# A conditional residual matmul on one core: results stored from a ring of their own, four rows to a partition, and plain copies in place of the residual add

## The chip, the core and the metric

The kernel runs on one core of one Trainium2 chip. The metric is the device time of one execution in microseconds (us), lower is better. Three runs of the kernel before gave a median of 323.65 us.

## The reference

`x` is float32 of shape (128, 128, 1024): 128 samples, 128 channels C, 1024 time steps T. Every sample names one of 8 subjects, and each subject has a 128x128 float32 matrix.

```python
w = weights[subjects]                        # (B, C, D), subjects in 0 .. 7
out = x + jnp.einsum('bct,bcd->bdt', x, w)   # B = C = D = 128, T = 1024
```

The traffic that can't be avoided is 67.1 MB read and 67.1 MB written.

## The kernel before

Two samples (a = 0, 1) make a **tile**: the 64 low partitions (LOW) hold sample a = 0, the 64 high ones (HIGH) sample a = 1, and each partition holds two neighbouring channels of T values (R = 2, a run of 8 KB). Two tiles make a **pair**, which one load of 2 MB brings (line 98) and one store of 2 MB takes away (line 205); there are 64 tiles and 32 pairs. `x_ring` has 12 tile slots, so 6 pairs.

TensorE multiplies a tile in 16 matmuls of 64 rows by 512 columns (line 222): two halves of T, two channels r of each partition, two samples a. The product of sample a lies in its own PSUM tensor of 128x1024 float32, four banks; `product` holds two tiles (PRODUCTS = 2), which is all of PSUM. The columns of the weights are permuted (`bank`, lines 113 and 174), so that the 128 output rows come out as even channels in one half of the partitions and odd ones in the other. This matches two rows to a partition in the store.

The residual is split in two. Where an output row stands in the partitions in which its own x row stands, VectorE (DVE) adds x to the product (`sums`, lines 139 and 140). Where it stands in the other half, x can't be added in place; there the weights hold one more on the diagonal (`add_eye`, line 119), so that TensorE's product is already x plus the einsum, and ScalarE (ACT) only copies it (`cross`, lines 182 and 183). Both write the result over x in `x_ring`. DVE also copies the weights of each tile from `weight_bank` to `weight_ring` (`pick`, line 132), four tiles ahead.

The order is written out by hand, with semaphores. SyncE's queue (SP) issues loads; from the seventh pair on each waits until the store of the pair that had its slots has landed (`x_out`, line 95). ACT issues a pair's store behind its copies, once its own copies and DVE's sums are done (`whole`, lines 187 and 188). TensorE starts tile t when both engines are done with tile t - 2 (`summed`, `copied`) and the load of its pair is in (`x_in`). The first two and the last four tiles are stored one by one, 1 MB each (line 202).

Of the kernel before, what the change touches and what calls it, by code (L numbers as in the profile page):

```python
# [6 lines left out]
DMA_INC = 16  # L7
SLOTS = 12
PAIR = 2
LOADS_AHEAD = 4  # L10
PICK_AHEAD = 4
PRODUCTS = 2


def subject_residual_kernel(nc, x, subjects, weights, out):

# [8 lines left out]
    f32, i32 = mybir.dt.float32, mybir.dt.int32  # L25
    B, C, T = x.shape
    S, _, D = weights.shape
    assert C == D == nc.NUM_PARTITIONS
    H, R = C // 2, 2
    TILES = B // 2  # L30
    LAPS, REST = divmod(TILES, SLOTS)
    assert LAPS and SLOTS % PRODUCTS == 0 and REST % PRODUCTS == 0 and REST == PICK_AHEAD > PRODUCTS
    PAIRS, PAIR_SLOTS = TILES // PAIR, SLOTS // PAIR
    assert SLOTS % PAIR == 0 and REST % PAIR == 0 and LOADS_AHEAD < PAIR_SLOTS
    BANKS = T // PSUM_BANK_COLS

    SINGLE = (*range(PAIR), *range(TILES - REST, TILES))
# [3 lines left out]
    def stores(pairs, place):  # L41

        return sum(PAIR if (pair * PAIR_SLOTS + place) * PAIR in SINGLE else 1 for pair in range(pairs))

    LOW, HIGH = slice(0, H), slice(H, C)
    EVEN, ODD = slice(0, H), slice(H, D)
# [4 lines left out]
    out_of_pair = out.rearrange("(n j a) (h r) t -> n (a h) j (r t)", j=PAIR, a=2, r=R)  # L51

    with ExitStack() as ctx:  # L53
        x_ring = ctx.enter_context(nc.sbuf_tensor("x_ring", [C, SLOTS, R, T], f32))

# [14 lines left out]
        eye_low = ctx.enter_context(nc.semaphore("eye_low"))  # L70
        eye_high = ctx.enter_context(nc.semaphore("eye_high"))
        bank_low = ctx.enter_context(nc.semaphore("bank_low"))
        eyes_added = ctx.enter_context(nc.semaphore("eyes_added"))
# [3 lines left out]
        x_out = [ctx.enter_context(nc.semaphore(f"x_out{s}")) for s in range(PAIR_SLOTS)]  # L77
# [5 lines left out]
        summed = ctx.enter_context(nc.semaphore("summed"))  # L83

        copied = ctx.enter_context(nc.semaphore("copied"))
        block = ctx.enter_context(nc.Block())

        @block.sync
        def _(sp):
            sp.dma_start(weight_halves[:, :, :, :],  # L90
                         weights.rearrange("(i a) (h r) d -> (a h) i (r d)", a=2, r=R)).then_inc(weights_in, DMA_INC)
            for pair in range(PAIRS):
                lap, place = divmod(pair, PAIR_SLOTS)
                if lap:
                    sp.wait_ge(x_out[place], stores(lap, place) * DMA_INC)
                elif place >= LOADS_AHEAD:
                    sp.wait_ge(x_in[place - LOADS_AHEAD], DMA_INC)
# [3 lines left out]
        def _(pool):  # L101
            pool.memset(eye[:, :], 0.0).then_inc(eye_zero, 1)  # L102
            pool.wait_ge(eye_zero, 1)
            for begin, made in ((0, eye_low), (H, eye_high)):
                half = slice(begin, begin + H)
                pool.affine_select(eye[half, :], eye[half, :], pattern=[[-1, H]], base=0, channel_multiplier=1,  # L106
                                   compare_op=mybir.AluOpType.not_equal, fill=1.0).then_inc(made, 1)

        @block.vector
        def _(dve):  # L110
            def bank(half, source, subjects_of):

                return dve.tensor_copy(  # L113
                    weight_bank[half, subjects_of, :, :].rearrange("h i r (q k) -> h i r q k", q=2),
                    weight_halves[source, :, :, :].rearrange("h i r (k q) -> h i r q k", q=2))

            def add_eye(half, row, columns):
                cells = weight_bank[half, :, row, columns]
                return dve.tensor_tensor(cells, cells, eye[half, :].rearrange("h (s k) -> h s k", s=1).broadcast_to(  # L119
                    (H, S, H)), add)  # L120

            def subjects_of(tile):

                _, numbers = nc.values_load_multi_w_load_instructions(  # L124
                    subject_row[0:1, tile * 2:(tile + PICK_AHEAD) * 2], engines=(mybir.EngineType.DVE,), min_val=0,
                    max_val=S - 1, skip_runtime_bounds_check_because="DVE has clamped subject_row to 0 .. S - 1")
                return numbers

            def pick(slot, numbers):

                for subject, half in zip(numbers, (LOW, HIGH)):
                    done = dve.tensor_copy(weight_ring[half, slot, :, :], weight_bank[half, bass.ds(subject, 1), :, :])  # L132
                return done

            def sums(tile, slot):

                low, high = product[slot % PRODUCTS]
                dve.wait_ge(multiplied, tile + 1)
                dve.tensor_tensor(x_ring[LOW, slot, 0, :], low[LOW, :], x_ring[LOW, slot, 0, :], add)  # L139
                dve.tensor_tensor(x_ring[HIGH, slot, 1, :], high[HIGH, :], x_ring[HIGH, slot, 1, :], add).then_inc(summed, 1)  # L140

            dve.sem_inc(summed, PRODUCTS)
            dve.wait_ge(subjects_in, DMA_INC)
            dve.tensor_scalar(subject_row[0:1, :], subject_row[0:1, :], 0, S - 1, mybir.AluOpType.max,  # L144
                              mybir.AluOpType.min).then_inc(clamped, 1)
            dve.wait_ge(weights_in, DMA_INC)
            bank(LOW, LOW, EVENS)
            bank(LOW, HIGH, ODDS).then_inc(bank_low, 1)
            dve.wait_ge(eye_low, 1)
            dve.wait_ge(bank_low, 1)  # L150
            add_eye(LOW, 1, ODD)
            dve.wait_ge(eye_high, 1)
            dve.wait_ge(bank_high, 1)  # L153
            add_eye(HIGH, 0, EVEN).then_inc(eyes_added, 1)
            dve.wait_ge(eyes_added, 1)
            dve.wait_ge(clamped, 1)
            numbers = subjects_of(0)
            for tile in range(PICK_AHEAD):
                pick(tile, numbers[tile * 2:tile * 2 + 2]).then_inc(picked, 1)


            for tile in range(TILES):
                sums(tile, tile % SLOTS)
                ahead = tile + PICK_AHEAD
                if ahead < TILES:
                    if ahead % PICK_AHEAD == 0:
                        numbers = subjects_of(ahead)
                    own = ahead % PICK_AHEAD * 2
                    pick(ahead % SLOTS, numbers[own:own + 2])

        @block.scalar
        def _(act):
            def bank(half, source, subjects_of):
                return act.copy(  # L174
                    weight_bank[half, subjects_of, :, :].rearrange("h i r (q k) -> h i r q k", q=2),
                    weight_halves[source, :, :, :].rearrange("h i r (k q) -> h i r q k", q=2))

            def cross(tile, slot):

                low, high = product[slot % PRODUCTS]  # L180
                act.wait_ge(multiplied, tile + 1)
                act.copy(x_ring[LOW, slot, 1, :], low[HIGH, :])  # L182
                act.copy(x_ring[HIGH, slot, 0, :], high[LOW, :]).then_inc(copied, 1)  # L183

            def whole(tile):

                act.wait_ge(copied, tile + (PRODUCTS + 1))
                act.wait_ge(summed, tile + (PRODUCTS + 1))  # L188
# [3 lines left out]
            act.sem_inc(copied, PRODUCTS)  # L192
            act.wait_ge(weights_in, DMA_INC)
            bank(HIGH, LOW, EVENS)
            bank(HIGH, HIGH, ODDS).then_inc(bank_high, 1)
            for tile in range(TILES):
                slot = tile % SLOTS
                place, j = divmod(slot, PAIR)
                cross(tile, slot)
                if tile in SINGLE:  # L200
                    whole(tile)
                    act.dma_start(out_of_pair[tile // PAIR, :, j, :], x_ring[:, slot, :, :]).then_inc(x_out[place], DMA_INC)
                elif j == PAIR - 1:
                    whole(tile)
                    act.dma_start(out_of_pair[tile // PAIR], x_ring[:, place * PAIR:(place + 1) * PAIR, :, :]).then_inc(
                        x_out[place], DMA_INC)
            for place in reversed(range(PAIR_SLOTS)):
                act.wait_ge(x_out[place], DMA_INC * stores(LAPS + (place < REST // PAIR), place))

        @block.tensor  # L210
        def _(pe):
            def multiply(tile, slot, landed):

                pe.wait_ge(summed, tile + 1)
                pe.wait_ge(copied, tile + 1)
# [10 lines left out]

# [21 lines left out]
```

## Time and profile before

| | us |
|---|---|
| median of 3 runs (323.53 to 324.3) | 323.65 |
| profiled execution, its own time | 323.31 |
| its span, first to last instruction | 321.5 |
| TensorE matmuls busy, 1024 | 243.8 |
| DVE busy, 261 instructions | 196.3 |
| ACT busy, 131 instructions | 132.2 |
| moved by DMA, 134.83 MB, mean | 419 GB/s |
| GpSimd (POOL) busy, 7 instructions | 0.8 |

The span is what the trace covers; the profiled execution's own time is 1.81 us longer, and the median another 0.34 us above that. In the rows below an instruction reads as line, engine, operation, output<-input, partitions x elements, count. "ACTq" and "SPq" rows are the queues' own work, here the issuing of a DMA. A DMA's time in the chain of waits runs from its issue to its landing, so it holds the time that it queued behind other transfers.

### The profile page before, as it was taken

Reading aid. Unit: us, or ns where it says so; the run is one execution under the profiler, and the core shown is the slowest. Engines: PE = TensorE matmul, PEld = TensorE weight load, DVE = VectorE, ACT = ScalarE, POOL = GpSimd, SP = SyncE. Lnnn points to the kernel's source line nnn. Section 1 sums busy time; section 2 is a strip of 40 time slices with the busy share of each in tenths; the row PEclk is TensorE's granted clock in tenths of the full one; section 3 lists DMA queues with packets and bytes.
Section 4 is the critical chain, followed back from the end, with each engine's and each line's share of the span. In section 5 each row is a group of like instructions: output and inputs, shape, how many; then the busy total and the mean of one; then the engine's idle time right before and its main releaser. Section 6 shows DMA issues by size and latency. Waiting matters only on the chain.

```text
span 321.5 us, 2871 instructions
## 1 busy us (share of the span) xinstructions
PE 243.8 (76%) x1024; PEld 112.7 (35%) x1024; DVE 196.3 (61%) x261; ACT 132.2 (41%) x131; POOL 0.8 (0%) x7
## 2 busy tenths in 40 slices
PE   0799997878687866779868698666986868876650
PEld 0344442334343432334424244333333434443320
DVE  3288888637657555764757737567463774755560
ACT  4056566324444242542425525335342553443450
POOL 1000000000000000000000000000000000000000
PEclk9999999979989997997979979998897998999995
DMA  7999999999999999999999999999999999999996
GB/s 287 422 411 427 421 428 425 428 429 429 425 428 428 428 426 428 428 427 427 428 429 428 426 427 430 428 425 428 430 427 426 426 431 428 426 425 432 421 428 271
DMA packets 18024, 134.83 MB, mean 419 GB/s; under 512 B 1105, under 2 KB 1633, under 8 KB 1633
## 3 DMA queue, kind: packets, MB, share of 16 engines
q1 hardware_dynamic: 9232, 67.64, 50.2%
q10 hardware_dynamic: 8784, 67.12, 49.4%
q8 instruction: 2, 0.03, 0.0%
q14 instruction: 6, 0.04, 0.0%
HBM read 67.64 MB, written 67.11 MB: 419 GB/s over the span
## 4 chain that ended last, share of the span: by engine, by line
DMA 73%; PE 17%; DVE 3%; issue 3%; DVEq 1%; ACT 1%; ACTq 0%
DMA out<-x_ring 37%; DMA x_ring<-x 34%; PE product L222 17%; DVE x_ring L140 2%; DMA weight_halves<-weights 1%; ACT weight_bank L174 1%; DVE x_ring L139 1%; DVEq L53 0%; DVEq L124 0%; DVEq L132 0%; DVE weight_bank L119 0%; DVE weight_ring L132 0%; ACTq L188 0%; DVEq L153 0%
## 5 line engine op out<-in xcount | busy, mean ns | idle before, releaser
L222 PE MATMUL product<-x_ring,weight_ring 64*128 64x512 f32 x1024 | 243.8, 630 | 66.1 <-DMA x_ring<-x 43.2
L222 PEld LDWEIGHTS product<-x_ring,weight_ring 64*128 64x128 f32 x1024 | 112.7, 199 | 196.4 <-issue 123.2
L139 DVE TENSOR_TENSOR x_ring<-product,x_ring 64x1024 f32<-64x1024 f32 x64 | 77.9, 1217 | 106.6 <-PE product L222 106.6
L182 ACT COPY x_ring<-product 64x1024 f32<-64x1024 f32 x64 | 64.5, 1008 | 175.5 <-PE product L222 175.5
L140 DVE TENSOR_TENSOR x_ring<-product,x_ring 64x1024 f32<-64x1024 f32 x64 | 78.6, 1228 | 0.8
L183 ACT COPY x_ring<-product 64x1024 f32<-64x1024 f32 x64 | 64.2, 1003 | 0.8
L132 DVE COPY weight_ring<-weight_bank 64x256 f32 x128 | 36.9, 288 | 3.9 <-issue 1.0
L174 ACT COPY weight_bank<-weight_halves 64x1024 f32<-64x1024 f32 x2 | 2.2, 1115 | 2.1 <-DMA weight_halves<-weights 2.1
L144 DVE TENSOR_SCALAR subject_row<-subject_row 1x128 int32<-1x128 int32 x1 | 0.2, 215 | 3.6 <-DMA subject_row<-subjects 3.6
L113 DVE COPY weight_bank<-weight_halves 64x1024 f32<-64x1024 f32 x2 | 1.4, 688 | 0.9 <-DMA weight_halves<-weights 0.9
L174 ACT ACT_TABLE_LOAD x1 | 1.3, 1283 | 1.3 <-PEq L240 1.3
L119 DVE TENSOR_TENSOR weight_bank<-weight_bank,eye 64x512 f32<-64x512 f32 x2 | 1.4, 686 | 0.3 <-ACT weight_bank L174 0.2
L106 POOL TENSOR_SCALAR_AFFINE_SELECT eye<-eye 64x64 f32<-64x64 f32 x2 | 0.5, 234 | 0.3 <-POOL eye L102 0.2
L102 POOL MEMSET eye<- 128x64 f32 x1 | 0.2, 151 | 0.3 <-POOLq L240 0.3
L240 POOL MEMSET const-float32-0.0<- 128x1 f32 x1 | 0.1, 98 | 0.2 <-issue 0.2
L240 POOL MEMSET const-float32-1.0<- 128x1 f32 x1 | 0.1, 98 | 0.0
L240 POOL MEMSET const-bfloat16-1.0<- 128x1 bf16 x1 | 0.1, 98 | 0.0
L240 POOL MEMSET const-uint8-127<- 128x1 uint8 x1 | 0.1, 98 | 0.0
## 6 DMA issues: line engine op xcount, KB each, us to landing
x_ring<-x SPq DMA_DIRECT2D x32, 2048.0 KB, 22.0
out<-x_ring ACTq DMA_DIRECT2D x29, 2048.0 KB, 26.2
out<-x_ring ACTq DMA_DIRECT2D x6, 1024.0 KB, 10.6
weight_halves<-weights SPq DMA_DIRECT2D x1, 512.0 KB, 3.9
subject_row<-subjects ACTq DMA_DIRECT2D x1, 8.0 KB, 2.8
```

Of the source, the lines that this page charges most:

```text
L102: pool.memset(eye[:, :], 0.0).then_inc(eye_zero, 1)
L106: pool.affine_select(eye[half, :], eye[half, :], pattern=[[-1, H]], base=0, channel_multiplier=1, compare_op=mybir.AluOpType.not_equal, fi ...
L113: return dve.tensor_copy(weight_bank[half, subjects_of, :, :].rearrange("h i r (q k) -> h i r q k", q=2), weight_halves[source, :, :, :].r ...
L119: return dve.tensor_tensor(cells, cells, eye[half, :].rearrange("h (s k) -> h s k", s=1).broadcast_to((H, S, H)), add)
L132: done = dve.tensor_copy(weight_ring[half, slot, :, :], weight_bank[half, bass.ds(subject, 1), :, :])
L139: dve.tensor_tensor(x_ring[LOW, slot, 0, :], low[LOW, :], x_ring[LOW, slot, 0, :], add)
L140: dve.tensor_tensor(x_ring[HIGH, slot, 1, :], high[HIGH, :], x_ring[HIGH, slot, 1, :], add).then_inc(summed, 1)
L174: return act.copy(weight_bank[half, subjects_of, :, :].rearrange("h i r (q k) -> h i r q k", q=2), weight_halves[source, :, :, :].rearrang ...
L182: act.copy(x_ring[LOW, slot, 1, :], low[HIGH, :])
L183: act.copy(x_ring[HIGH, slot, 0, :], high[LOW, :]).then_inc(copied, 1)
L222: last = pe.matmul(product[slot % PRODUCTS][a][:, cols], weight_ring[half, slot, r, :], x_ring[half, slot, r, cols], start=r == 0, stop=r ...
L240: nc = bacc.Bacc("TRN2", target_bir_lowering=False, num_devices=1)
```

## The change

- `x_ring` shrinks to 10 tile slots (5 pairs). A new ring, `results`, holds 6 pairs of results, [128, 6, 4, 1024] float32.
- A result pair lies with four channels to a partition (Q = 4), 32 partitions to a sample, so a store of 2 MB takes a run of 16 KB from each of 128 partitions. All pairs are stored whole, the first and the last too.
- The weights get one more on the whole diagonal (one eye of 64 columns for both r, added into `weight_halves` before `bank`), so that x is nowhere added afterwards.
- A tile's product is then taken from PSUM in 8 plain copies of 32 partitions x 1024 columns (a = 0, 1; q = 0 to 3). ACT takes the first 4 of an even tile and the first 5 of an odd one, DVE the other 4 or 3.
- The picking of weights moves from DVE to GpSimd. It runs 5 pairs ahead, held back by `multiplied`.
- A load waits on `picked`, which itself waits on `multiplied` of the pair that had the slots; it waits on no store any more. What waits on a store (`pair_out`) is the first copy of a pair, on ACT and on DVE, from the seventh pair on.

```diff
-SLOTS = 12
+SLOTS = 10
-PICK_AHEAD = 4
+RESULTS = 6
...
+    BLOCKS = [(a, q) for a in range(2) for q in range(Q)]
+    ACT_BLOCKS = (4, 5)
...
-    out_of_pair = out.rearrange("(n j a) (h r) t -> n (a h) j (r t)", j=PAIR, a=2, r=R)
+    out_of_pair = out.rearrange("(n g) (k q) t -> n (g k) (q t)", g=PAIR * 2, q=Q)
...
+        results = ctx.enter_context(nc.sbuf_tensor("results", [C, RESULTS, Q, T], f32))
...
+        def target(tile, a, q):
+
+            pair, j = divmod(tile, PAIR)
+            g = j * 2 + a
+            return results[g * K:(g + 1) * K, pair % RESULTS, q, :]
+
+        def rows(tile, a, q):
+
+            return product[tile % PRODUCTS][a][q * K:(q + 1) * K, :]
 
         @block.sync
...
-                    sp.wait_ge(x_out[place], stores(lap, place) * DMA_INC)
+
+                    sp.wait_ge(picked, (pair + 1) * PAIR)
...
+            for pair in range(PAIRS):
+                if pair % 2 == 0:
+                    numbers = subjects_of(pair)
+                if pair == 0:
+                    pool.wait_ge(bank_low, 1)
+                    pool.wait_ge(bank_high, 1)
+                elif pair >= PAIR_SLOTS:
+                    pool.wait_ge(multiplied, (pair - PAIR_SLOTS + 1) * PAIR)
+                for j in range(PAIR):
+                    slot = pair * PAIR % SLOTS + j
+                    for a, half in enumerate((LOW, HIGH)):
+                        done = pool.tensor_copy(weight_ring[half, slot, :, :],
+                                                weight_bank[half, bass.ds(numbers[(pair % 2 * PAIR + j) * 2 + a], 1), :, :])
+                    done.then_inc(picked, 1)
 
         @block.vector
...
+            dve.wait_ge(eye_made, 2)
+            add_eye(0)
+            add_eye(1).then_inc(eyes_added, 1)
+            dve.wait_ge(eyes_added, 1)
             bank(LOW, LOW, EVENS)
             bank(LOW, HIGH, ODDS).then_inc(bank_low, 1)
...
             for tile in range(TILES):
...
+                pair = tile // PAIR
+                dve.wait_ge(multiplied, tile + 1)
+                if tile % PAIR == 0 and pair >= RESULTS:
+                    dve.wait_ge(pair_out[pair % RESULTS], pair // RESULTS * DMA_INC)
...
+                for a, q in BLOCKS[ACT_BLOCKS[tile % 2]:]:
+                    last = dve.tensor_copy(target(tile, a, q), rows(tile, a, q))
+                last.then_inc(dve_copied, 1)
 
         @block.scalar
...
+                act.wait_ge(multiplied, tile + 1)
+                if j == 0 and pair >= RESULTS:
+                    act.wait_ge(pair_out[place], pair // RESULTS * DMA_INC)
+                for a, q in BLOCKS[:ACT_BLOCKS[tile % 2]]:
+                    last = act.copy(target(tile, a, q), rows(tile, a, q))
+                last.then_inc(act_copied, 1)
+                if j == PAIR - 1:
+                    act.wait_ge(act_copied, tile + (PRODUCTS + 1))
+                    act.wait_ge(dve_copied, tile + (PRODUCTS + 1))
+                    act.dma_start(out_of_pair[pair], results[:, place, :, :]).then_inc(pair_out[place], DMA_INC)
```

What follows shows the order of instructions on an engine, line and operation, output and input, and the semaphores that it waits for. First ACT, one whole pair in the middle of the program, before the change (`copied` and `summed` count the tiles that ACT and DVE have finished):

```order
L182 COPY x_ring<-product_0 64x1024 [waits multiplied]
L183 COPY x_ring<-product_1 64x1024
L182 COPY x_ring<-product_0 64x1024 [waits multiplied]
L183 COPY x_ring<-product_1 64x1024
L205 DMA out<-x_ring 128x2x2048 [waits summed,copied]
```

And ACT for one pair of the changed kernel, the first one that reuses a place of `results`:

```order
L197 COPY results<-product_0 32x1024 [waits pair_out0,multiplied]
L197 COPY results<-product_0 32x1024 x3
L197 COPY results<-product_0 32x1024 [waits multiplied]
L197 COPY results<-product_0 32x1024 x3
L197 COPY results<-product_1 32x1024
L202 DMA out<-results 128x4096 [waits dve_copied,act_copied]
```

Four copies of 1024 columns ahead of a store became nine, and the store still stands behind the last of them and ahead of the next pair's first copy.

The second place is DVE in the steady part, one tile before the change (an ISA row readies the register that names the subject):

```order
L139 TENSOR_TENSOR x_ring<-product_0,x_ring 64x1024 [waits multiplied]
L140 TENSOR_TENSOR x_ring<-product_1,x_ring 64x1024
L132 ISA
L132 COPY weight_ring<-weight_bank 64x256
L132 ISA
L132 COPY weight_ring<-weight_bank 64x256
```

And one pair of the changed kernel on DVE:

```order
L174 COPY results<-product_1 32x1024 [waits pair_out0,multiplied]
L174 COPY results<-product_1 32x1024 x3
L174 COPY results<-product_1 32x1024 [waits multiplied]
L174 COPY results<-product_1 32x1024 x2
```

DVE's two sums and two picks a tile became four or three copies; the picks now stand on GpSimd, four to a pair.

## Rows read from the trace of the kernel before

**Rows 1.** The page: what the DMA engines moved in 40 equal slices

```profile
GB/s 287 422 411 427 421 428 425 428 429 429 425 428 428 428 426 428 428 427 427 428 429 428 426 427 430 428 425 428 430 427 426 426 431 428 426 425 432 421 428 271
```

**Rows 2.** Stretches: length, busy us (count) per engine, PE clock, DMA share, GB/s

```profile
0.00:4.00 4.00, 0.00 (x0) 0.00 (x0) 0.21 (x1) 1.28 (x1) 0.82 (x7) 1.00 0.53 142
...
120.00:160.00 40.00, 31.36 (x132) 14.46 (x130) 24.15 (x33) 16.07 (x17) 0.00 (x0) 0.91 1.01 428
...
312.00:316.00 4.00, 0.00 (x0) 0.00 (x0) 0.39 (x1) 0.00 (x0) 0.00 (x0) 0.51 1.01 426
316.00:321.50 5.50, 0.00 (x0) 0.00 (x0) 0.00 (x0) 0.00 (x0) 0.00 (x0) 0.50 0.48 201
```

**Rows 3.** The chain that ended last, one lap of the ring: start, us, what

```profile
66.06 27.48 DMA out<-x_ring
93.57 21.44 DMA x_ring<-x
115.05 7.16 PE product L222 x32
```

**Rows 4.** Groups by form: count, busy us, mean ns of one, idle before

```profile
L140 DVE TENSOR_TENSOR x_ring<-product,x_ring 64x1024 f32<-64x1024 f32 x64 | 78.6, 1228 | 0.8
L182 ACT COPY x_ring<-product 64x1024 f32<-64x1024 f32 x64 | 64.5, 1008 | 175.5 <-PE product L222 175.5
L183 ACT COPY x_ring<-product 64x1024 f32<-64x1024 f32 x64 | 64.2, 1003 | 0.8
L132 DVE COPY weight_ring<-weight_bank 64x256 f32 x128 | 36.9, 288 | 3.9 <-issue 1.0
L119 DVE TENSOR_TENSOR weight_bank<-weight_bank,eye 64x512 f32<-64x512 f32 x2 | 1.4, 686 | 0.3 <-ACT weight_bank L174 0.2
L106 POOL TENSOR_SCALAR_AFFINE_SELECT eye<-eye 64x64 f32<-64x64 f32 x2 | 0.5, 234 | 0.3 <-POOL eye L102 0.2
L144 DVE TENSOR_SCALAR subject_row<-subject_row 1x128 int32<-1x128 int32 x1 | 0.2, 215 | 3.6 <-DMA subject_row<-subjects 3.6
```

**Rows 5.** Timeline of ACT and DVE, 225 to 262: start, us, what

```profile
241.54 1.01 ACT L182 COPY x_ring<-product 64x1024 f32<-64x1024 f32 x1 [1.41 <-PE product L222]
242.56 1.00 ACT L183 COPY x_ring<-product 64x1024 f32<-64x1024 f32 x1
...
254.01 1.23 DVE L140 TENSOR_TENSOR x_ring<-product,x_ring 64x1024 f32<-64x1024 f32 x1
...
255.33 0.38 ACTq L205 DMA_DIRECT2D out<-x_ring  x1
257.56 1.01 ACT L182 COPY x_ring<-product 64x1024 f32<-64x1024 f32 x1 [2.75 <-PE product L222]
```

**Rows 6.** Timeline of PE, pairs of tiles: start, us, count, [idle before]

```profile
66.22 8.83 PE L222 MATMUL product<-x_ring,weight_ring 64*128 64x512 f32 x32 [2.75 <-DMA x_ring<-x]
105.37 7.14 PE L222 MATMUL product<-x_ring,weight_ring 64*128 64x512 f32 x32 [2.66 <-DMA x_ring<-x]
253.82 7.14 PE L222 MATMUL product<-x_ring,weight_ring 64*128 64x512 f32 x32 [1.07 <-DMA x_ring<-x]
```

**Rows 7.** Timeline of the start: start, us, what, [idle before]

```profile
0.73 0.42 SPq L90 DMA_DIRECT2D weight_halves<-weights  x1
0.74 0.44 ACTq L190 DMA_DIRECT2D subject_row<-subjects  x1
1.29 1.28 ACT L174 ACT_TABLE_LOAD   x1 [1.29 <-PEq L240]
4.69 2.24 ACT L174 COPY weight_bank<-weight_halves 64x1024 f32<-64x1024 f32 x2 [2.12 <-DMA weight_halves<-weights]
10.39 14.19 PE L222 MATMUL product<-x_ring,weight_ring 64*128 64x512 f32 x53 [10.39 <-DVE weight_ring L132]
16.48 1.01 ACT L182 COPY x_ring<-product 64x1024 f32<-64x1024 f32 x1 [9.56 <-PE product L222]
```

**Rows 8.** Timeline of the end: the issue of the last store

```profile
312.48 0.34 ACTq L202 DMA_DIRECT2D out<-x_ring  x1
```

More of the change, by code:

```diff
@@ L28, in subject_residual_kernel @@
     assert C == D == nc.NUM_PARTITIONS
-    H, R = C // 2, 2
+    R, Q = 2, 4
+    H, K = C // R, D // Q
     TILES = B // 2
     LAPS, REST = divmod(TILES, SLOTS)
-    assert LAPS and SLOTS % PRODUCTS == 0 and REST % PRODUCTS == 0 and REST == PICK_AHEAD > PRODUCTS
+    assert LAPS and SLOTS % PRODUCTS == 0 and REST % PRODUCTS == 0
     PAIRS, PAIR_SLOTS = TILES // PAIR, SLOTS // PAIR
-    assert SLOTS % PAIR == 0 and REST % PAIR == 0 and LOADS_AHEAD < PAIR_SLOTS
+    assert SLOTS % PAIR == 0 and REST % PAIR == 0 and LOADS_AHEAD < PAIR_SLOTS and PAIR * 2 * K == C
     BANKS = T // PSUM_BANK_COLS
-    SINGLE = (*range(PAIR), *range(TILES - REST, TILES))
     SUBJECT_ROWS = 16
-    def stores(pairs, place):
-        return sum(PAIR if (pair * PAIR_SLOTS + place) * PAIR in SINGLE else 1 for pair in range(pairs))
+    BLOCKS = [(a, q) for a in range(2) for q in range(Q)]
+    ACT_BLOCKS = (4, 5)
     LOW, HIGH = slice(0, H), slice(H, C)
-    EVEN, ODD = slice(0, H), slice(H, D)
     EVENS, ODDS = slice(0, S, 2), slice(1, S, 2)
@@ L69, in subject_residual_kernel @@
         eye_zero = ctx.enter_context(nc.semaphore("eye_zero"))
-        eye_low = ctx.enter_context(nc.semaphore("eye_low"))
-        eye_high = ctx.enter_context(nc.semaphore("eye_high"))
+        eye_made = ctx.enter_context(nc.semaphore("eye_made"))
+        eyes_added = ctx.enter_context(nc.semaphore("eyes_added"))
         bank_low = ctx.enter_context(nc.semaphore("bank_low"))
-        eyes_added = ctx.enter_context(nc.semaphore("eyes_added"))
         bank_high = ctx.enter_context(nc.semaphore("bank_high"))
         x_in = [ctx.enter_context(nc.semaphore(f"x_in{s}")) for s in range(PAIR_SLOTS)]
-        x_out = [ctx.enter_context(nc.semaphore(f"x_out{s}")) for s in range(PAIR_SLOTS)]
+        pair_out = [ctx.enter_context(nc.semaphore(f"pair_out{s}")) for s in range(RESULTS)]
         picked = ctx.enter_context(nc.semaphore("picked"))
         multiplied = ctx.enter_context(nc.semaphore("multiplied"))
-        summed = ctx.enter_context(nc.semaphore("summed"))
-        copied = ctx.enter_context(nc.semaphore("copied"))
+        dve_copied = ctx.enter_context(nc.semaphore("dve_copied"))
+        act_copied = ctx.enter_context(nc.semaphore("act_copied"))
         block = ctx.enter_context(nc.Block())
+        def target(tile, a, q):
[4 more added lines that the diff above has]
+            return product[tile % PRODUCTS][a][q * K:(q + 1) * K, :]
         @block.sync
@@ L101, in _, with subjects_of @@
         def _(pool):
+            def subjects_of(pair):
+                _, numbers = nc.values_load_multi_w_load_instructions(
+                    subject_row[0:1, pair * PAIR * 2:(pair + 2) * PAIR * 2], engines=(mybir.EngineType.Pool,), min_val=0,
+                    max_val=S - 1, skip_runtime_bounds_check_because="DVE has clamped subject_row to 0 .. S - 1")
+                return numbers
             pool.memset(eye[:, :], 0.0).then_inc(eye_zero, 1)
             pool.wait_ge(eye_zero, 1)
-            for begin, made in ((0, eye_low), (H, eye_high)):
-                half = slice(begin, begin + H)
+            for half in (LOW, HIGH):
@@ L106, in _ @@
                 pool.affine_select(eye[half, :], eye[half, :], pattern=[[-1, H]], base=0, channel_multiplier=1,
[L107 removed]
+                                   compare_op=mybir.AluOpType.not_equal, fill=1.0).then_inc(eye_made, 1)
+            pool.wait_ge(clamped, 1)
+            for pair in range(PAIRS):
[12 more added lines that the diff above has]
+                    done.then_inc(picked, 1)
@@ L109, in _, with add_eye @@
         @block.vector
         def _(dve):
+            def add_eye(r):
+                cells = weight_halves[:, :, r, slice(r, D, R)]
+                return dve.tensor_tensor(cells, cells, eye[:, :].rearrange("h (s k) -> h s k", s=1).broadcast_to(
+                    (C, S // 2, H)), add)
             def bank(half, source, subjects_of):
                 return dve.tensor_copy(
-                    weight_bank[half, subjects_of, :, :].rearrange("h i r (q k) -> h i r q k", q=2),
-                    weight_halves[source, :, :, :].rearrange("h i r (k q) -> h i r q k", q=2))
@@ L117, in add_eye @@
[L117 to L140, printed above, removed]
@@ L142, in _ @@
-            dve.sem_inc(summed, PRODUCTS)
+                    weight_bank[half, subjects_of, :, :].rearrange("h i r (q k) -> h i r q k", q=Q),
+                    weight_halves[source, :, :, :].rearrange("h i r (k q) -> h i r q k", q=Q))
+            dve.sem_inc(dve_copied, PRODUCTS)
             dve.wait_ge(subjects_in, DMA_INC)
@@ L146, in _ @@
             dve.wait_ge(weights_in, DMA_INC)
+            dve.wait_ge(eye_made, 2)
+            add_eye(0)
+            add_eye(1).then_inc(eyes_added, 1)
+            dve.wait_ge(eyes_added, 1)
             bank(LOW, LOW, EVENS)
             bank(LOW, HIGH, ODDS).then_inc(bank_low, 1)
[L149 to L159, printed above, removed]
-            for tile in range(TILES):
[L163 to L169, printed above, removed]
+            for tile in range(TILES):
+                pair = tile // PAIR
+                dve.wait_ge(multiplied, tile + 1)
+                if tile % PAIR == 0 and pair >= RESULTS:
+                    dve.wait_ge(pair_out[pair % RESULTS], pair // RESULTS * DMA_INC)
+                if tile + PRODUCTS < SLOTS:
+                    dve.wait_ge(picked, tile + (PRODUCTS + 1))
+                for a, q in BLOCKS[ACT_BLOCKS[tile % 2]:]:
+                    last = dve.tensor_copy(target(tile, a, q), rows(tile, a, q))
+                last.then_inc(dve_copied, 1)
         @block.scalar
@@ L174, in bank @@
                 return act.copy(
[L175 to L188, printed above, removed]
+                    weight_bank[half, subjects_of, :, :].rearrange("h i r (q k) -> h i r q k", q=Q),
+                    weight_halves[source, :, :, :].rearrange("h i r (k q) -> h i r q k", q=Q))
             act.dma_start(subject_row[:, :], subjects.rearrange("(one b) -> one b", one=1).broadcast_to(
                 (SUBJECT_ROWS, B))).then_inc(subjects_in, DMA_INC)
-            act.sem_inc(copied, PRODUCTS)
-            act.wait_ge(weights_in, DMA_INC)
+            act.sem_inc(act_copied, PRODUCTS)
+            act.wait_ge(eyes_added, 1)
             bank(HIGH, LOW, EVENS)
@@ L196, in _ @@
             for tile in range(TILES):
[L197 to L208, printed above, removed]
+                pair, j = divmod(tile, PAIR)
+                place = pair % RESULTS
+                act.wait_ge(multiplied, tile + 1)
[8 more added lines that the diff above has]
+                    act.dma_start(out_of_pair[pair], results[:, place, :, :]).then_inc(pair_out[place], DMA_INC)
+            for place in range(RESULTS):
+                act.wait_ge(pair_out[place], DMA_INC * len(range(place, PAIRS, RESULTS)))
         @block.tensor
@@ L212, in multiply @@
             def multiply(tile, slot, landed):
-                pe.wait_ge(summed, tile + 1)
-                pe.wait_ge(copied, tile + 1)
+                pe.wait_ge(dve_copied, tile + 1)
+                pe.wait_ge(act_copied, tile + 1)
                 if slot % PAIR == 0:
```

## The prediction

> **What bounds the kernel now.** I read the 40 slices first. From the second slice to the 39th the DMA engines move 411 to 432 GB/s, some 427 on average, and in stretches their busy share is all of the time [rows 1, 2]. The reader is to see that no long stretch stands out: the 134.8 MB of the page at 427 GB/s take 315.8 us of the 321.5, and the other 5.7 us lie at both ends, before the first bytes move and behind the last. The chain says the same in another way: a place of the ring goes through store (27.48), load (21.44) and two tiles on TensorE (7.16), and with the handshakes in between that is 58.9 us for six pairs, 9.8 us a pair [rows 3]. 4.19 MB at 427 GB/s are 9.82 us. So DMA bounds it, and the engines wait: per pair TensorE needs 7.14 us when its clock is up [rows 6], DVE 4 sums and 4 picks, 4 x 1.22 + 4 x 0.29 = 6.0, and ACT four copies, 4.0 [rows 4]. The question is which of these passes 9.8 us after the change, and what happens at the end, where nothing is left to load.
>
> **ACT, the term that decides.** The change turns ACT's four copies of 64 partitions into nine of 32 partitions, each still 1024 columns. The trace has no copy of 32 partitions. What it shows is that time goes with columns: one partition by 128 took 0.215 us on DVE, 64 partitions by 256 took 0.288 [rows 4], 128 times the data for a third more time. So I take the 64-partition copy's own time, 1.00 us, and its pitch in the timeline: 241.54 to 242.56, 1.02 us from one start to the next [rows 5]. Nine copies: 8 x 1.02 + 1.00 = 9.16 us. Then the store: it waits for ACT's own last copy (before, 254.01 + 1.23 = 255.24 to 255.33, so 0.09 us), its issue holds ACT's queue 0.34 us (the form with one run per partition), and behind an issue the queue came to its next instruction 0.11 us later (0.74 + 0.44 = 1.18, then 1.29) [rows 5, 7, 8]. Nothing of this can hide: behind the issue stand the next pair's copies, and the issue can't go before the last copy is complete. A pair costs ACT P = 9.16 + 0.09 + 0.34 + 0.11 = **9.70 us**. The bounds: copies at 1.00 with no handshake but the issue, 9.4; a pitch of 1.03 and 0.6 us between pairs, 9.85.
>
> The Trainium skill, VectorE: DVE Perf Modes, section on the TRN2 errata, counts a ScalarE instruction from PSUM to SBUF as 172 cycles plus its columns at 1.2 GHz, with no term for partitions. That is 0.997 us for 1024 columns, against 1.003 and 1.008 in the rows; an estimate from that page is P = 9 x 0.997 + 0.54 = 9.51. It speaks against this change, since 32 partitions cost as much as 64.
>
> **Does another engine come before ACT?** DVE copies 3.5 blocks a tile. A copy reads no second input, so it is at most the 1.22 us of the sum; four picks of 256 columns are 4 x 0.288 = 1.15, and with the fixed part counted once and not four times it may be 1.0: 7.0 to 8.5 us a pair, under 9.70 [rows 4]. TensorE needs 6.9 to 7.1. A product's loop: from TensorE's start to the copy's start 3.74 us (253.82 to 257.56), four DVE copies 4.9 at most, and back: 8.7 us for two tiles; for the odd tile 3.74 + 5.1 = 8.8 [rows 4 to 6]. All under 9.70, so ACT runs without a gap; TensorE is ready 0.9 to 1.0 us before ACT comes to a tile. GpSimd's four picks lie between DVE's 0.29 us and four times its own 64-column operation, 0.94 [rows 4]: 1.2 to 3.8 us a pair, and each is issued five pairs ahead. They cost nothing in the steady part, and would from 2.4 us a pick. DVE's sums and picks that go away were not on the path, and give nothing.
>
> **Loads and stores.** A load is issued when TensorE is done with the pair five before, some 40 us before it is needed. DMA has 9.82 us of work in 9.70 us, so it falls behind by 0.12 us a pair, 3 us over 27 loads: loads arrive in time and the place in `results`, six pairs or 58 us, is free. So DMA is just full until the last load is in. Then comes what costs: from pair 27 on only stores are left, 4.9 us of transfer a pair, while ACT still takes 9.70. Before, the transfers queued up ahead of the end and kept DMA full until 3 us before it; now it idles for half of the last five pairs.
>
> **The start.** Weights are in at 4.69. The diagonal comes first now, two sums of 256 columns, half of the 0.686 us row each, then ACT's two bank copies of 2.24 us in all: 4.69 + 0.7 + 0.1 + 2.24 = 7.7. Four picks (1.2 to 3.8) and the 0.4 us that TensorE took to start bring 9.3 to 11.9, against 10.39 before. I leave it at 10.39, and the first copy at 16.48 [rows 4, 7]; the bounds are -1 and +1.5 us.
>
> **The end.** The last store is now 2 MB by itself. First bytes moved 1.94 us behind the first issue (0.57 MB in the first 4 us are 1.33 us at 427, so from 2.67, and the issue is at 0.73) [rows 2, 7]; 2.10 MB take 4.91; and behind the last byte came 2.92 us (before: from 312.48 to 321.5 are 9.02 us, in which 1.50 + 1.11 MB moved, 6.10 us) [rows 2, 8]. Together 9.77; the bounds are 8.3 and 9.8, since part of the two waits may be one.
>
> **The sum.** Span = 16.48 + 31 x 9.70 + 9.16 + 0.09 + 9.77 = 336.2 us, or 32 P + 25.8. Against the profiled execution's own span of 321.5 that is +14.7; with the 1.81 us around the span 338.0, and with the 0.34 us by which the median stood above that execution **338.3 us**, 4.5% slower.
>
> **Rivals.** *ACT as the bound, and TensorE's clock on top (0.15).* Before, TensorE started at half its clock in 9 of 32 pairs, each time behind an idle time of 2.5 us or more; such a pair, the first at 66.22, took 8.83 us in place of 7.14, and behind 1.07 us none did [rows 6]. The changed kernel leaves TensorE 2.8 us idle a pair, in two gaps of about 1.2 and 1.6, which speaks against it; other idle times of 2.66 left the clock up too. If nine tiles start slow all the same, each costs the 1.69 us less the 0.9 to 1.05 of slack: 6 to 7 us, 344 to 346 us.
>
> *The other side: copies of 32 partitions are cheaper, and DMA stays the bound (0.05).* It decides at one point: 32 P + 25.8 + 2.15 is 323.65 at P = 9.24, that is at a pitch of 0.97 us instead of 1.02. If a copy went with its data it would take 0.5 us; the DVE rows of 1 and 64 partitions speak against it. Then the sum is DMA's: 134.8 MB at 427 to 432 GB/s (the best slice, if 16 KB runs gave it everywhere) plus 5.7 us are 317.8 to 321.5, so 320 to 323.6 us, 321.8 in the middle. The trace shows no run of 16 KB. By the Trainium skill, DMA: Bandwidth & Descriptors, section on why small descriptors are slow, each packet costs about 3 cycles beside one per 32 bytes; an estimate from it is 0.3% of all traffic, 1 us, and only where DMA is the bound.
>
> *Stores of 16 KB runs move worse (0.06).* If the rate fell to the 411 GB/s of the worst slice [rows 1], a pair would be 10.2 us of DMA, 0.5 us over ACT's, and after 27 pairs loads would be 14 us behind; the 40 us by which they run ahead cover that. What it costs is a fuller queue at the end, 337 to 342 us. Below 390 GB/s DMA would be the bound again, at 134.8 / 0.39 + 5.7 = 351.
>
> *No change that can be told (0.02)*, if small savings in every handshake came together.
>
> **How the numbers follow.** ACT as the bound alone has 0.72: P from 9.5 to 9.85 with the bounds of start and end gives 329.8 + 2.15 - 1 - 1.5 = 329.5 at the very least, some 332 without all of them at once, and 341 + 2.15 + 1.5 = 344.7 at most. With the clock's case the range is 331 to 346. Measurement of this kernel can tell 0.3% from no change. Faster: most of the rival on the other side, 0.04. Same: 0.03. Slower: 0.93.
>
> **What would show it.** In the profile after: ACT busy about 288 x 1.0 = 290 us, over 85% of the span; 9.7 us from a pair's first copy to the next pair's; ACT's idle behind the store's issue about 0.5 us, and hardly any wait for TensorE; TensorE waiting for ACT instead of DMA, at a clock near 1.00; GB/s of 425 to 430 until about 285 us and then about half. The prediction is wrong if a 32-partition copy on ACT takes much less than 1.0 us, if the mean over the whole span stays near 419 GB/s, or if DVE's copies take over 1.4 us, since then DVE would be the bound.

## The result, and the profile after

The changed kernel takes 333.25 us (median of 4 runs, 332.89 to 333.62) against 323.59 us for the one before, measured together: a ratio of 1.0295, with a 95% interval of 1.0275 to 1.0316. It is slower by 3%. The forecast was 338.3 us in a range of 331 to 346. Two single executions further down, of 338.00 us with the 4 KB runs (one of 6) and of 628.83 us with the end cut as before (one of 12), count as disturbed and are left out of the ratios, though not out of the medians. The profiled execution took 333.19 us, its span is 331.4.

The page of the changed kernel: its first line, and what DMA moved in 40 equal slices.

```profile
span 331.4 us, 3183 instructions
GB/s 285 423 421 430 424 422 430 436 427 422 435 428 434 419 428 431 430 429 437 414 428 431 440 419 435 417 441 414 431 436 420 430 433 421 439 422 279 221 255 253
```

Up to the 36th slice, 298 us, it reads like [rows 1]. The last four slices, 33 us, move 252 GB/s in the mean, 0.6 of the rate before. The costliest groups of the same page (count, busy us, mean ns of one, idle before and what ended it):

```profile
L197 ACT COPY results<-product 32x1024 f32<-32x1024 f32 x288 | 288.9, 1003 | 25.8 <-ACT results L197 14.2
L174 DVE COPY results<-product 32x1024 f32<-32x1024 f32 x224 | 273.7, 1222 | 41.0 <-PE product L217 28.2
L217 PE MATMUL product<-x_ring,weight_ring 64*128 64x512 f32 x1024 | 238.9, 605 | 80.0 <-ACT results L197 47.1
L136 POOL COPY weight_ring<-weight_bank 64x256 f32 x128 | 51.1, 399 | 220.0 <-PE product L217 206.9
L180 ACT COPY weight_bank<-weight_halves 64x1024 f32<-64x1024 f32 x2 | 4.0, 1996 | 3.3 <-DVE weight_halves L144 3.2
L149 DVE COPY weight_bank<-weight_halves 64x1024 f32<-64x1024 f32 x2 | 2.1, 1060 | 0.0
```

A copy of 32 partitions takes ACT 1003 ns, to the nanosecond what 64 partitions took at L183 [rows 4]. On DVE it takes 1222 ns, what the residual add of twice as many partitions took (1228). ACT is busy 294.2 us of the 331.4 (all its groups), and TensorE's waits, which were for DMA, are for ACT. One pair in the middle of the timeline:

```profile
103.82 0.34 ACTq L202 DMA_DIRECT2D out<-results  x1
103.93 3.70 PE L217 MATMUL product<-x_ring,weight_ring 64*128 64x512 f32 x16 [1.42 <-ACT results L197]
104.25 9.13 ACT L197 COPY results<-product 32x1024 f32<-32x1024 f32 x9 [0.47 <-ACT results L197]
108.54 3.70 PE L217 MATMUL product<-x_ring,weight_ring 64*128 64x512 f32 x16 [0.91 <-ACT results L197]
113.42 0.34 ACTq L202 DMA_DIRECT2D out<-results  x1
```

Nine copies run without a gap for 9.13 us, ACT waits 0.47 us for its own last copy and the issue, and the next pair begins: 9.60 us. This repeats to the end. The start:

```profile
5.03 0.76 DVE L144 TENSOR_TENSOR weight_halves<-weight_halves,eye 128x256 f32<-128x256 f32 x2 [0.87 <-DMA weight_halves<-weights]
5.83 4.00 ACT L180 COPY weight_bank<-weight_halves 64x1024 f32<-64x1024 f32 x2 [3.24 <-DVE weight_halves L144]
12.25 9.23 PE L217 MATMUL product<-x_ring,weight_ring 64*128 64x512 f32 x32 [12.25 <-POOL weight_ring L136]
18.09 9.13 ACT L197 COPY results<-product 32x1024 f32<-32x1024 f32 x9 [8.26 <-PE product L217]
```

And the end, in stretches with the columns of [rows 2]; the last store is issued at 324.62.

```profile
300.00:310.00 10.00, 7.41 (x32) 3.36 (x33) 8.95 (x8) 9.40 (x11) 0.00 (x0) 1.00 0.70 297
310.00:320.00 10.00, 7.41 (x32) 3.31 (x32) 8.95 (x8) 9.43 (x10) 0.00 (x0) 1.00 0.53 221
...
324.00:325.00 1.00, 0.00 (x0) 0.00 (x0) 0.00 (x0) 0.59 (x1) 0.00 (x0) 0.50 0.00 0
325.00:326.00 1.00, 0.00 (x0) 0.00 (x0) 0.00 (x0) 0.00 (x0) 0.00 (x0) 0.50 0.61 262
...
330.00:331.40 1.40, 0.00 (x0) 0.00 (x0) 0.00 (x0) 0.00 (x0) 0.00 (x0) 0.50 0.01 0
```

Before the last store moves, DMA stands still. ACT sets the pace to the end, and DMA has nothing left but one store a pair.

### The profile page after: what moved, and what is told of

Its sections match the earlier page's. It is cut to its first block, busy times and chain, and to the rows that moved or that the text cites. A ratio compares the mean times of both kernels' runs of the same rounds, so it can differ in the third digit from the quotient of the medians.

```text
span 331.4 us, 3183 instructions
## 1 busy us (share of the span) xinstructions
PE 238.9 (72%) x1024; PEld 106.1 (32%) x1024; DVE 276.7 (84%) x229; ACT 294.2 (89%) x291; POOL 51.9 (16%) x135
## 4 chain that ended last, share of the span: by engine, by line
ACT 80%; issue 11%; ACTq 3%; PE 2%; DMA 1%; POOLq 0%; DVE 0%; POOL 0%
ACT results L197 79%; ACTq L202 3%; PE product L217 2%; DMA weight_halves<-weights 1%; ACT weight_bank L180 1%; DVE weight_halves L144 0%; POOL weight_ring L136 0%; ACTq L195 0%; POOLq L114 0%; POOLq L136 0%; POOLq L130 0%
## 5 line engine op out<-in xcount | busy, mean ns | idle before, releaser
L197 ACT COPY results<-product 32x1024 f32<-32x1024 f32 x288 | 288.9, 1003 | 25.8 <-ACT results L197 14.2
L174 DVE COPY results<-product 32x1024 f32<-32x1024 f32 x224 | 273.7, 1222 | 41.0 <-PE product L217 28.2
L217 PE MATMUL product<-x_ring,weight_ring 64*128 64x512 f32 x1024 | 238.9, 605 | 80.0 <-ACT results L197 47.1
L217 PEld LDWEIGHTS product<-x_ring,weight_ring 64*128 64x128 f32 x1024 | 106.1, 188 | 211.9 <-issue 169.1
L136 POOL COPY weight_ring<-weight_bank 64x256 f32 x128 | 51.1, 399 | 220.0 <-PE product L217 206.9
L180 ACT COPY weight_bank<-weight_halves 64x1024 f32<-64x1024 f32 x2 | 4.0, 1996 | 3.3 <-DVE weight_halves L144 3.2
L149 DVE COPY weight_bank<-weight_halves 64x1024 f32<-64x1024 f32 x2 | 2.1, 1060 | 0.0
L144 DVE TENSOR_TENSOR weight_halves<-weight_halves,eye 128x256 f32<-128x256 f32 x2 | 0.8, 424 | 0.9 <-DMA weight_halves<-weights 0.9
```

Of the source, the lines that this page charges most:

```text
L136: done = pool.tensor_copy(weight_ring[half, slot, :, :], weight_bank[half, bass.ds(numbers[(pair % 2 * PAIR + j) * 2 + a], 1), :, :])
L144: return dve.tensor_tensor(cells, cells, eye[:, :].rearrange("h (s k) -> h s k", s=1).broadcast_to((C, S // 2, H)), add)
L149: return dve.tensor_copy(weight_bank[half, subjects_of, :, :].rearrange("h i r (q k) -> h i r q k", q=Q), weight_halves[source, :, :, :].r ...
L174: last = dve.tensor_copy(target(tile, a, q), rows(tile, a, q))
L180: return act.copy(weight_bank[half, subjects_of, :, :].rearrange("h i r (q k) -> h i r q k", q=Q), weight_halves[source, :, :, :].rearrang ...
L197: last = act.copy(target(tile, a, q), rows(tile, a, q))
```

## The experiments

Ratios are to the kernel before, on the same chip, with 95% intervals. All experiments start from the changed kernel.

**1. Stores issued by SyncE's queue.**

```diff
+            def store(pair):
+                sp.wait_ge(act_copied, pair * PAIR + PAIR - 1 + (PRODUCTS + 1))
+                sp.wait_ge(dve_copied, pair * PAIR + PAIR - 1 + (PRODUCTS + 1))
+                sp.dma_start(out_of_pair[pair], results[:, pair % RESULTS, :, :]).then_inc(pair_out[pair % RESULTS], DMA_INC)
...
                 sp.dma_start(x_ring[:, place * PAIR:(place + 1) * PAIR, :, :], x_of_pair[pair]).then_inc(x_in[place], DMA_INC)
+                if pair >= PAIR_SLOTS:
+                    store(pair - PAIR_SLOTS)
...
-                    act.dma_start(out_of_pair[pair], results[:, place, :, :]).then_inc(pair_out[place], DMA_INC)
```

> The changed kernel with its stores issued by SyncE's queue, each behind the load of the pair five later. Theory (ACT's queue is the bound: nine copies, a handshake, the issue, 9.60 us a pair): ACT's pair falls to 9.13 + 0.05 = 9.18 us; ACT would end at 18.1 + 31 x 9.18 + 9.13 = 312 and the span at 319, while 134.84 MB at 429 GB/s plus 5.7 us at both ends are 320. So DMA is the bound again, 320 to 324 us of span, a measured time of 322 to 326. Rival (the ring of five pairs and loads held back by the picks make the loss): nothing of that is changed, it stays at 330 or more.

325.19 us, ratio 1.0042 (1.003 to 1.0055). ACT's copies are the same 288; its idle time is gone:

```profile
L208 ACT COPY results<-product 32x1024 f32<-32x1024 f32 x288 | 288.9, 1003 | 13.1 <-PE product L222 9.0
```

Idle before the copies fell from 25.8 to 13.1 us, most of it the wait at the start. A pair takes ACT 9.16 us, it ends at 311.8 us, and DMA moves 423 to 433 GB/s from 20 us to 310: it is the bound again. The theory stands: 0.44 us less a pair took 8 of the 9.7 us away. Of the rest, 0.4%, experiment 7 tells more.

**2. Two rows to a partition in the results.** Four copies of 64 partitions a tile, two on each engine, and runs of 8 KB. The rings, the whole diagonal and the picks on GpSimd stay.

```diff
-    R, Q = 2, 4
+    R, Q = 2, 2
...
-    ACT_BLOCKS = (4, 5)
+    ACT_BLOCKS = (2, 2)
...
-    out_of_pair = out.rearrange("(n g) (k q) t -> n (g k) (q t)", g=PAIR * 2, q=Q)
+    out_of_pair = out.rearrange("(n j a) (h r) t -> n (a h) j (r t)", j=PAIR, a=2, r=R)
```

> The changed kernel with two rows to a partition in its results, so four copies of 64 partitions a tile, two on ACT and two on DVE, and runs of 8 KB; the rings, the whole diagonal and the picks on GpSimd stay. Theory (the count of copies is the cost): ACT 4 x 1.02 + 0.5 = 4.6 and DVE 4.9 us a pair, DMA is the bound, 321 to 325 us. It also starts some 1.7 us earlier, since the copies of the bank read every second column and not every fourth. Rival (rings, loads behind the picks, picks on GpSimd): 330 or more.

323.52 us, ratio 0.9992 (0.9984 to 1.0001): no different from before. From its page:

```profile
L173 DVE COPY results<-product 64x1024 f32<-64x1024 f32 x128 | 156.6, 1223 | 148.2 <-PE product L216 147.4
L196 ACT COPY results<-product 64x1024 f32<-64x1024 f32 x128 | 129.0, 1008 | 174.5 <-PE product L216 173.8
L179 ACT COPY weight_bank<-weight_halves 64x1024 f32<-64x1024 f32 x2 | 2.2, 1108 | 3.1 <-DVE weight_halves L143 3.1
```

Twice the partitions in the same time, so 129 us of copies in place of 289. The ring of its own, the ring of five pairs, the loads behind the picks, the picks on GpSimd and the whole diagonal are all in this kernel, and cost nothing that shows in its time. The bank copies are back at 1108 ns, and TensorE starts at 10.34 instead of 12.25.

**3. and 4. Other shares of the 16 copies of a pair**, `ACT_BLOCKS = (4, 4)` and `(5, 5)`; one run each.

> The changed kernel with four copies of every tile on ACT and four on DVE. Theory (ACT and DVE are both close to the bound, and the fuller one sets the pair): ACT 8.6 us a pair, DVE 8 x 1.23 = 9.84, so DVE sets it: 18.1 + 32 x 9.84 + 6.9 = 339.9 of span, 341.7 us. Rival (ACT's queue alone is the bound): one copy less on every second tile gives back up to 1.0 us a pair, DMA is the bound, 323.

> The changed kernel with five copies of every tile on ACT and three on DVE. Theory (a copy more a pair on ACT is 1.016 us a pair): P = 10.62, 18.1 + 31 x 10.62 + 10.15 + 6.8 = 364.3 of span, 366.1 us. Rival (DMA or the loads set the pair, ACT only follows): little change, 333 to 338.

344.07 and 366.83 us, spans 342.3 and 364.9. Store issues of the first, then of the second:

```profile
107.53 0.34 ACTq L202 DMA_DIRECT2D out<-results  x1
117.44 0.34 ACTq L202 DMA_DIRECT2D out<-results  x1
```

```profile
103.09 0.34 ACTq L202 DMA_DIRECT2D out<-results  x1
113.70 0.34 ACTq L202 DMA_DIRECT2D out<-results  x1
```

9.91 us a pair with eight copies on DVE, 10.61 with ten on ACT. The second is the forecast to 0.2%; the first lies 2.4 us over it, 0.07 us a pair that DVE spends besides its copies (8 x 1.23 = 9.84). Both rivals fall. Of these shares nine and seven is the best; nine on ACT alone are 9.13 us, eight on DVE 9.84, so no other share of sixteen such copies gets a pair below this.

**5. The issue behind two copies of the next pair.** ACT still issues the stores.

```diff
-                for a, q in BLOCKS[:ACT_BLOCKS[tile % 2]]:
+                for n, (a, q) in enumerate(BLOCKS[:ACT_BLOCKS[tile % 2]]):
+                    if n == 2 and j == 0 and pair:
+                        store(pair - 1)
                     last = act.copy(target(tile, a, q), rows(tile, a, q))
...
```

> The changed kernel with ACT still issuing the stores, but each behind the first two copies of the next pair, when the copies that it waits for are long done. Theory A (the issue costs only because ACT's engine runs dry while the queue waits for the last copy; with copies already handed to the engine the 0.34 us hide under them): ACT's pair is 9.16 us as with SyncE's stores, DMA the bound, 324 to 326 us. Rival B (the issue always stops ACT's copies for its 0.34 us): only the 0.13 us of handshake go, 9.47 us a pair, 18.1 + 31 x 9.47 + 9.1 + 6.8 = 327.6 of span, 329.4 us or a little more.

329.69 us, ratio 1.0193 (1.0178 to 1.0208): the time is the rival's, the mechanism is not. Its timeline at 100 us and at 190:

```profile
99.61 2.02 ACT L205 COPY results<-product 32x1024 f32<-32x1024 f32 x2
100.64 0.34 ACTq L187 DMA_DIRECT2D out<-results  x1
...
101.65 9.14 ACT L205 COPY results<-product 32x1024 f32<-32x1024 f32 x9
...
190.02 8.83 PE L222 MATMUL product<-x_ring,weight_ring 64*128 64x512 f32 x32 [3.21 <-DMA x_ring<-x]
```

The issue, 100.64 to 100.98, lies under a running copy (the two last from 99.61 to 101.63), and a pair takes 9.15 us, 100.64 to 109.79. So theory A is right about ACT. But from 178 us on TensorE waits for x, six times, 14.5 us in all, which neither theory had. The landing times point to the cause. DMA issues by line (count, KB each, median us from issue to landing), this run first, then the changed kernel, then the one before:

```profile
x_ring<-x SPq DMA_DIRECT2D x32, 2048.0 KB, 33.3
out<-results ACTq DMA_DIRECT2D x32, 2048.0 KB, 11.7
```

```profile
x_ring<-x SPq DMA_DIRECT2D x32, 2048.0 KB, 24.3
out<-results ACTq DMA_DIRECT2D x32, 2048.0 KB, 11.7
```

```profile
x_ring<-x SPq DMA_DIRECT2D x32, 2048.0 KB, 22.0
out<-x_ring ACTq DMA_DIRECT2D x29, 2048.0 KB, 26.2
```

My reading is that the two queues take turns run by run: since stores have runs of 16 KB and loads of 8 KB, a store lands in less than half the time it took before, at the cost of the loads. The next two runs test that.

**6. Late issue with the store cut in two; and stores in runs of 4 KB.** The first cuts each store of experiment 5 by channels into two of 1 MB with 8 KB runs; the second cuts each store of experiment 2 into two of 1 MB with 4 KB runs.

```diff
-                act.dma_start(out_of_pair[pair], results[:, pair % RESULTS, :, :]).then_inc(
+                for part in range(2):
+                    act.dma_start(out_of_pair[pair, :, part * 2 * T:(part + 1) * 2 * T],
+                                  results[:, pair % RESULTS, part * 2:(part + 1) * 2, :]).then_inc(
...
```

> As the run with the late issue, but every store is cut into two of 1 MB with runs of 8 KB, both issued at the same place. Theory (loads and stores lie in two queues that take turns run by run, so stores of 16 KB runs get two thirds of DMA while both have work: they land in 11.7 us, loads take 33.3, and from 170 us on TensorE waits for x): with equal runs a load lands sooner and a store later, both 18 to 30 us, the waits for x of 14.5 us mostly go, 324.5 to 326.5 us. Rival (ACT's queue gives the loads their delay, or the x ring of five pairs is too short at 9.15 us a pair whatever the runs): loads stay near 33 us, 329 to 330.

> Two rows to a partition, every store cut into two of 1 MB with runs of 4 KB, loads unchanged at 8 KB. Theory (turns run by run): now loads get two thirds of DMA, a load lands in less than the 38.7 us of the run with 8 KB stores, and a store takes longer than its 31.1 us, 35 to 50; the rate is 0.5% to 1% lower for the shorter runs, 323.5 to 326 us. Rival (the queues share by bytes): both landings as before.

The cut stores: 324.72 us, ratio 1.0033 (1.0021 to 1.0046), 5 us less than uncut, though ACT's queue holds twice the issues. Landings:

```profile
x_ring<-x SPq DMA_DIRECT2D x32, 2048.0 KB, 20.4
out<-results ACTq DMA_DIRECT2D x64, 1024.0 KB, 24.4
```

Loads land in 20.4 us instead of 33.3, and no wait for x is left. The rival falls. The cut also doubled the number of stores, so by itself it doesn't single out the length of the runs; the DMA packets recorded in the traces do. Added up for each microsecond from 60 to 280 in which both queues move data, the stores have a median share of the bytes of 0.67 in the changed kernel and 0.66 in experiment 5 (16 KB runs), 0.49 with the cut stores, and 0.50 in the kernel before and in experiment 2, whose stores are whole with 8 KB runs.

The 4 KB runs took 334.53 us, ratio 1.0312 (1.0289 to 1.0334), far beyond the forecast. Landings with 8 KB runs (experiment 2), then with 4 KB:

```profile
x_ring<-x SPq DMA_DIRECT2D x32, 2048.0 KB, 38.7
out<-results ACTq DMA_DIRECT2D x32, 2048.0 KB, 31.1
```

```profile
x_ring<-x SPq DMA_DIRECT2D x32, 2048.0 KB, 13.3
out<-results ACTq DMA_DIRECT2D x64, 1024.0 KB, 29.1
GB/s 290 423 421 422 422 425 427 425 425 359 369 407 421 379 427 425 397 388 403 359 428 423 420 383 410 425 424 421 379 422 425 426 421 409 424 422 420 421 392 230
```

Loads come down from 38.7 to 13.3 us, and the stores' share while both queues move is 0.33, as turns by runs say and sharing by bytes does not. A store was to take 35 to 50 us and took 29.1. The time was mis-forecast too, and the trace shows where it goes. From ACT's timeline, and a stretch with the columns of [rows 2]:

```profile
211.34 13.23 ACTq L202 DMA_DIRECT2D out<-results  x2
224.67 4.07 ACT L196 COPY results<-product 64x1024 f32<-64x1024 f32 x4 [13.36 <-issue]
78.00:80.00 2.00, 2.00 (x7) 0.80 (x4) 0.00 (x0) 0.46 (x1) 0.00 (x0) 0.50 1.04 244
```

The issues themselves hold ACT's queue: 0.87 us each in the median, up to 12.84, and 147 us for all 64, where the 32 of experiment 2 take 0.38 each. The next pair's copies stand behind them. They don't wait for a place in `results`: the store that frees it had always landed 15 us or more before the copy. While ACT stands still TensorE comes to a stop as well and loads run out, so that for 58 of the 220 us from 60 to 280 stores move alone, at 376 GB/s in the mean and as little as 244, with the DMA engines busy all the time (1.04 in the row above). Both queues together move 419. As an estimate, 58 x (1 - 376/428) + 162 x (1 - 419/428) = 10.4 us is lost against 428 GB/s, and this run is 11.0 us over experiment 2. Why the issues take so long and why runs of 4 KB move more slowly alone stays open.

**7. Stores from SyncE's queue with 8 KB runs, and the end cut as before.** The first is experiment 1 with the layout of experiment 2. The second is experiment 2 with the first pair and the last two stored tile by tile.

> Two rows to a partition (runs of 8 KB) and stores issued by SyncE's queue: beside the run with SyncE's stores and four rows it differs in the length of the runs and the count of copies alone, both of them with DMA as the bound. Theory (16 KB runs give about 0.2% of rate in the middle and lose it at the end, where the last transfers trickle): 323.0 to 324.0 us, so 1 to 2 us under the 325.2 with 16 KB runs. Rival (stores on SyncE's queue are what costs there): 325 here too.

> Two rows to a partition, stores from ACT, and the first pair and the last two pairs stored tile by tile, 1 MB each, as the kernel before does. Theory (behind the issue of a last store of 2 MB DMA trickles for about 1 us longer than behind one of 1 MB): 322.8 to 323.4 us, 0.3 to 0.7 us under the run with two rows and whole pairs. Rival (the end is the same however it is cut): 323.5.

The first: 324.92 us, ratio 1.0034 (1.0024 to 1.0044). Its interval and that of the 16 KB runs in experiment 1 overlap, so the times show no difference that goes with the length of the runs, and the theory's 1 to 2 us fall. With two rows to a partition, moving the stores from ACT's queue (0.9992) to SyncE's (1.0034) is what costs. But the two kernels with SyncE's stores differ in one thing more: with 8 KB runs SyncE's issues take 3.89 us for a store and 2.74 for a load in the median, with 16 KB runs 0.36 and 0.37, so that equal times need not have one cause. The second: 323.98 us, ratio 1.0008 (0.9999 to 1.0017), nothing gained by the cut. A part of the 0.3 to 0.4% of these kernels with one queue lies at the end, where DMA empties: from 310 us on, experiment 1 moves 416 GB/s for 5 us and takes 7.9 more to the end of the span, experiment 2 moves 429 and takes 7.1, though it has more left to move, 3.7 MB against 3.4. That is 0.8 us of span. Another 0.5 us of experiment 1 lie outside the span: its executions are 2.3 us longer than their spans, those of the kernel before 1.8. Why DMA empties more slowly stays open. The cut stores of experiment 6 lie on ACT's queue and have the 0.3% too, so it may be more than one cause.

No version beat the kernel before. All that are not held up by an engine end at its time or 0.3 to 0.4% above.

## Why the prediction was right

**ACT as the bound** was the forecast, and it was right in kind and nearly in size: 9.60 us a pair against 9.70. The copies took 9.13 of the 9.16, the handshake and the resumed queue 0.13 instead of 0.09 + 0.11. Over the run a pair took 9.59 us in the mean (the first few had 0.41 us between their copies), and up to the issue of the last store this makes the forecast 3.4 us too long. Columns set the time of a copy, not partitions: 1 x 128 against 64 x 256 on DVE had to stand for it before; L197 and experiment 2 show it directly. By the estimate of 9.51 us a pair from the Trainium skill, VectorE: DVE Perf Modes, section on the TRN2 errata, the sum would have been 332.3 us; the measured pair lies between the two.

**"Nothing of this can hide"** was true of the order as written, and wrong as a statement on the hardware. Experiment 5 hides the whole 0.34 us issue under copies that ACT's engine already has, and a pair takes 9.15 us. What costs is that the queue stands at a wait for ACT's own last copy while the engine runs dry.

**Other engines.** All stayed below ACT, as forecast: DVE at 8.6 us a pair (at most 8.5 forecast), GpSimd at 4 x 0.40 us, within its bounds, and TensorE at 2 x 3.70 = 7.4 (6.9 to 7.1). The clock's rival did not come: the mean granted clock was 0.988 against 0.938 before, with TensorE's idle time in gaps of 0.9 and 1.4 us.

**Loads and stores.** The rate in the middle, 427 to 430 GB/s over stretches of 40 us, hardly rose with runs of 16 KB. That DMA falls to about half once the loads are in is what the page shows, from about 300 us and not 285. The 285 was a misreading: "from pair 27 on only stores are left" counts a load as done when it is issued. In the trace the last load is issued at 272.8 us and landed at 305. The amounts give the time whichever queue goes first: 67.6 MB of loads are 158 us at 427 GB/s, a store every 9.6 us adds 4.9 us of work from 28 us on, and together they are done, as an estimate, at 300 us. A small slip besides: the lap of the chain is 58.7 us (from the store at 66.06 to the next one at 124.78), not 58.9; it is 9.8 us a pair either way.

**The start** was taken at no change, with +1.5 us as the bound, and came 1.6 us later, just outside, at 18.09. The term mis-sized is the bank copy. I had taken 2.24 us for two on ACT, and they took 4.00, since with Q = 4 they read every fourth column instead of every second; experiment 2 turns that back.

**The end** was 6.8 us from the issue, not 9.77. By its share this was the most mis-sized term. I had read the 1.94 us ahead of the first bytes off the start of the program, and the 2.92 us behind the last off an end at which several transfers were still under way. Here first bytes came some 0.8 us behind the issue, and 1.4 us passed behind the last.

So three terms were off, -3.4, +1.6 and -3.0 us, and their sum is the 4.8 us between the forecast span of 336.2 and the measured 331.4. That the late start made up for a part of the rest is luck.

**The other side.** A cheaper copy would have had to come below a pitch of 0.96 us (the 9.24 us less the 0.54 and the last copy's 1.00, over eight; the prediction has 0.97); it is 1.016. Faster needed P under 9.24; experiments 1 and 6, at 9.16 and 9.15, show that even then DMA gives no less than the time before.

## What to carry to other kernels

Count the instructions that a layout for DMA costs on the engines that fill it: a copy's time goes by its columns, so half the partitions means twice the copies. When a kernel is bound by DMA, compare whole sums and not only the steps. Here ACT's 9.60 us a pair were less than the 9.82 us that DMA needs for a pair's load and store, and the kernel was slower all the same, since ACT starts late and the last store comes behind it: 18.1 + 31 x 9.59 + 9.2 + 6.8 = 331.4 us of span, against the 321.5 of the kernel before, which DMA bounds. The handshakes and issues in an engine's queue count in its step; without them, at 9.16, DMA was the bound again. Put the issue of a store behind work that the engine already has, not behind a wait for its own last instruction.

## What the runs showed of the hardware

- Two DMA queues that both have work take turns by runs, not by bytes. Beside loads in runs of 8 KB, stores in runs of 16, 8 and 4 KB had 0.67, 0.50 and 0.33 of the bytes while both moved. Loads landed in a median of 33.3 us beside 16 KB runs and 20.4 beside 8 KB (experiments 5 and 6, ACT at the same pace), and in the other layout in 38.7 beside 8 KB and 13.3 beside 4 KB.
- Runs of 16 KB on half of the traffic gave no gain in time over runs of 8 KB: 1.0042 against 1.0034 with stores on SyncE's queue, where the long issues with 8 KB runs are a second difference.
- The length of an issue is not fixed. Its median was 0.34 to 0.41 us in most kernels here, but 0.87 in the median and up to 12.84 for stores in 4 KB runs on ACT's queue, and 3.89 for stores in 8 KB runs that share SyncE's queue with the loads (up to 11.33).
- A copy in SBUF that reads every fourth float32 took ACT 1996 ns and DVE 1060, against 1108 and 688 for every second: 64 x 1024 in all four.
- One DMA issue of 0.34 us on ACT's queue runs beside ACT's copies when these are already handed over: 9.15 us a pair against 9.60.
